# Expert adapter with layer norm: biases broadcast by DMA, W_up loaded by slots, W_down in 4 KB pieces, tail reordered

## The reference

```python
Wd = W_down[stream]; bd = b_down[stream]; Wu = W_up[stream]; bu = b_up[stream]
g = ln_w[stream]; b = ln_b[stream]
h = jnp.einsum('bsh,bhk->bsk', hidden_states, Wd) + bd[:, None, :]     # 512 -> 256
h = jax.nn.gelu(h, approximate=False)
h = jnp.einsum('bsk,bkh->bsh', h, Wu) + bu[:, None, :]                 # 256 -> 512
h = residual + h
mean = jnp.mean(h, axis=-1, keepdims=True)
var = jnp.mean(jnp.square(h - mean), axis=-1, keepdims=True)
h = (h - mean) * jax.lax.rsqrt(var + LN_EPS)
return h * g[:, None, :] + b[:, None, :]
```

## Time and profile before

| | before |
|---|---|
| median of three runs | 143.63 us (143.4 to 145.49) |
| profiled execution | 143.75 us, its span 142.0 us |
| TensorE busy | 126.5 us, 89% |
| VectorE busy | 112.3 us, 79% |
| GpSimd (POOL) busy | 100.9 us, 71% |
| ScalarE busy | 85.7 us, 60% |
| DMA | 21.93 MB, mean 154 GB/s |

### The profile page before, as it was taken

The page is one execution under the profiler, slowest core; times in us unless marked ns, Lnnn a source line. Parts: engine busy times, 40 slices in busy tenths (PEclk is TensorE's granted clock), DMA queues, the critical chain, the costliest instruction groups (busy, mean ns, idle before and its releaser), DMA issues.

```text
span 142.0 us, 4003 instructions
## 1 busy us (share of the span) xinstructions
PE 126.5 (89%) x814; PEld 109.8 (77%) x815; DVE 112.3 (79%) x269; ACT 85.7 (60%) x177; POOL 100.9 (71%) x110
## 2 busy tenths in 40 slices
PE   0399948999999999999999999999999999999800
PEld 0152947999989999898999999999999999998500
DVE  1764449588888888888898888888888978897982
ACT  0763556656666666666666666666766666665320
POOL 3000691055888988888889888888888898889670
PEclk9999999999999999999999999999999999999985
DMA  1959999834325355544553554544446533333346
GB/s 50 359 131 346 282 305 317 210 124 129 115 74 144 90 176 156 150 137 155 145 193 127 170 162 133 167 145 149 149 148 148 148 74 74 79 74 74 74 113 185
DMA packets 13185, 21.93 MB, mean 154 GB/s; under 512 B 2290, under 2 KB 3826, under 8 KB 13172
## 3 DMA queue, kind: packets, MB, share of 16 engines
q1 hardware_dynamic: 8948, 16.01, 39.0%
q10 hardware_dynamic: 4224, 5.79, 13.5%
HBM read 13.39 MB, written 8.65 MB: 155 GB/s over the span
## 4 chain that ended last, share of the span: by engine, by line
PE 83%; DVE 6%; POOL 2%; ACT 2%; DMA 2%; DVEq 1%; issue 1%; POOLq 1%; ACTq 0%
PE hg_ps L733 31%; PE y_ps L758 29%; PE xT_ps L721 10%; PE y_ps L699 5%; PE hg_ps L742 5%; DVE wu_lo L239 2%; POOL res L348 2%; DMA itok_all_i<-in_itok_B_dram 2%; PE hg_ps L695 2%; ACT normed L427 1%; DVEq L568 1%; POOLq L60 1%; ACT wu_hi L437 1%; PE hg_ps L699 1%; DVE hb L586 1%
## 5 line engine op out<-in xcount | busy, mean ns | idle before, releaser
L333 POOL TENSOR_TENSOR xb<-x_sb,bu_rows 128x512 f32<-128x512 f32 x33 | 43.5, 1319 | 13.8 <-ACT bu_rows L449 13.5
L348 POOL TENSOR_TENSOR res<-normed,lnb_rows 128x512 f32<-128x512 f32 x31 | 39.9, 1287 | 15.7 <-ACT normed L427 15.7
L407 ACT ACTIVATE g<-hb 128x256 f32<-128x256 f32 x33 | 13.8, 418 | 36.0 <-DVE hb L586 36.0
L598 DVE BATCH_NORM_STATS2 r_stats<-y_ps 128x6 f32<-128x512 f32 x33 | 23.0, 696 | 8.3 <-issue 7.5
L578 DVE TENSOR_TENSOR xT_lo<-xT_ps,xT_hi 128x512 fp32r<-128x512 f32 x33 | 22.8, 689 | 3.9 <-ACT xT_hi L402 3.9
L619 DVE SCALAR_TENSOR_TENSOR scaled<-y_ps,r_mv,lnw_rows 128x512 f32<-128x512 f32 x33 | 24.5, 743 | 0.1
L733 PE MATMUL hg_ps<-wd_hi,xT_hi 128*128 x132 | 24.2, 306 | 0.0
L758 PE MATMUL y_ps<-wu_hi,gT_hi 128*128 x66 | 23.4, 435 | 0.7 <-ACT gT_hi L412 0.7
L339 POOL TENSOR_TENSOR rstd<-var_eps,half_neg 128x1 f32<-128x1 f32 x33 | 18.5, 562 | 7.1 <-DVE var_eps L607 7.1
L427 ACT ACTIVATE normed<-scaled,rstd 128x512 f32<-128x512 f32 x31 | 22.4, 722 | 1.6 <-DVE scaled L619 1.6
L402 ACT CAST xT_hi<-xT_ps 128x512 fp32r<-128x512 f32 x33 | 18.8, 571 | 4.3 <-PE xT_ps L721 4.3
(11 more groups left out here) (71 smaller groups left out, 136.6 us busy)
## 6 DMA issues: line engine op xcount, KB each, us to landing
x_sb<-in_x_dram SPq DMA_DIRECT2D x66, 128.0 KB, 2.8
out_dram<-res ACTq DMA_DIRECT2D x33, 128.0 KB, 2.4
out_dram<-res SPq DMA_DIRECT2D x33, 128.0 KB, 2.4
wd<-in_L_cond_W_down_dram ACTq DMA_DIRECT2D x3, 512.0 KB, 4.5
wu<-in_L_cond_W_up_dram SPq DMA_DIRECT2D x3, 512.0 KB, 6.1
lnw_rows<-in_L_cond_ln_w_dram SPq DMA_DIRECT2D x1, 768.0 KB, 6.7
lnb_rows<-in_L_cond_ln_b_dram SPq DMA_DIRECT2D x1, 768.0 KB, 7.9
bd_flat<-in_L_cond_b_down_dram SPq DMA_DIRECT2D x1, 3.0 KB
```

Of the source, the lines that this page charges most:

```text
L333: pool.tensor_tensor(xb[:, c % DEEP, :], x_sb[:, c % FAR, :], bu_rows[:, ds(e * H, H)], ALU.add).then_inc(xb_ready, 1)
L348: pool.tensor_tensor(res[:, c % FAR, :], normed[:, c % PAR, :], lnb_rows[:, ds(e * H, H)], ALU.add).then_inc(res_ready, 1)
L598: dve.bn_stats(r_stats[:, c % DEEP, :], y_ps[c % YBANKS][:]).then_inc(stats_ready, 1)
```

## The change

- `b_down` and `b_up` are no longer loaded flat and spread by TensorE. Two DMAs write them to all 128 partitions, `bd_rows` behind W_up of the first slot, `bu_rows` behind x of tile 1. The `spread_row` matmuls and the five ACT copies are gone.
- W_up is loaded by slots: slot 0 gets the expert of the first tile, read from a table, slots 1 and 2 the ones behind it. TensorE's register table `up_down` holds a tile's slot and the next tile's expert. `up(0)` waits for slot 0 only, `up(1)` for all three.
- W_down is loaded as `(p c) n`, four consecutive rows (4 KB) to a partition, where it was `(c p) n`, four pieces of 1 KB. To match, `transpose_x` reads every fourth column of x, `k::KH`.
- TensorE sets the four `y_ps` banks with K=1 float32r matmuls, runs nine warm-ups before the first x transposes and one behind them; `down(0)` waits for the hi halves first and for the lo halves only where it uses them.
- In the sort, a tile's own expert is loaded by a DMA of its own (64 x 4 bytes) where it was taken out of the matrix by a masked sum; steps are reordered, and three small ones build the new tables.
- In the tail, VectorE scales the last tile ahead of `shift_last` of the one before; `last_places` (ACT) and `e_last` (VectorE, two entries for three) are read behind the main loop instead of ahead of it.

Declarations of tiles and semaphores are left out.

```diff
@@ -55,7 +55,7 @@
+    WARM_UPS_BEFORE, WARM_UPS_AFTER = 9, 1
 
@@ -222,10 +218,12 @@
         def load_w_down(eng, e):
-            eng.dma_start(wd[:, e, :, :], w_down[e].rearrange("(c p) n -> p c n", p=P)).then_inc(wd_in[e], 16)
-        def load_w_up(eng, e):
-            eng.dma_start(wu[:, e, :, :], w_up[e].rearrange("(c p) n -> p c n", p=P)).then_inc(wu_in[e], 16)
+            eng.dma_start(wd[:, e, :, :], w_down[e].rearrange("(p c) n -> p c n", p=P)).then_inc(wd_in[e], 16)
+        def load_w_up(eng, slot, e):
+            eng.dma_start(wu[:, slot, :, :], w_up[ds(e, 1), :, :].rearrange("a (c p) n -> p (a c) n", p=P)).then_inc(
+                wu_in[slot], 16)
@@ -243,8 +241,7 @@
         def _(sp):
-            sp.dma_start(bd_flat[:], rows_of(b_down, 1)).then_inc(bd_in, 16)
-            sp.dma_start(bu_flat[:], rows_of(b_up, 1)).then_inc(bu_in, 16)
+            sp.dma_start(itok_own_i[:], itok.rearrange("(p a) -> p a", a=1)).then_inc(itok_in, 16)
@@ -274,13 +271,22 @@
+            def entries_and_expert(t):
+                sp.reg_load(io_regs, io_table[0:1, ds(3 * t, 3)])
+                return ([sp.snap(reg, min_val=0, max_val=B - 1) for reg in io_regs[:2]],
+                        sp.snap(io_regs[2], min_val=0, max_val=E - t))
             load(0, 0, entries(0, 0, 2))
-            load_w_up(sp, 0)
-            load_w_up(sp, 1)
-            load(1, 1, entries(1, 0, 2))
-            load_w_up(sp, 2)
-            load(2, 2, entries(2, 0, 2))
-            load(3, 3, entries(3, 0, 2))
+            sp.wait_ge(slots_ready, 2)
+            for t in range(1, E + 1):
+                batches, e = entries_and_expert(t)
+                load_w_up(sp, t - 1, e + (t - 1))
+                if t == 1:
+                    sp.dma_start(bd_rows[:], rows_of(b_down, P)).then_inc(bd_in, 16)
+                load(t, t, batches)
+                if t == 1:
+                    sp.dma_start(bu_rows[:], rows_of(b_up, P)).then_inc(bu_in, 16)
@@ -310,11 +316,11 @@
-            pool.memset(ones_row[:], 1.0).then_inc(ones_ready, 1)
...
+            pool.iota(top_row[:], pattern=[[-1, E]], base=E - 1, channel_multiplier=0).then_inc(const_ready, 1)
@@ -348,7 +354,7 @@
-            pool.wait_ge(bu_ready, E)
+            pool.wait_ge(bu_in, 16)
             for t in range(DEEP):
@@ -362,9 +368,10 @@
             tiles(pool, body, FAR + 1, TILES - 1 - DEEP)
-            for t in range(TILES - DEEP, LAST):
-                shift(t - 1, t - 1)
-                power(t, t)
+            shift(LAST - 3, LAST - 3)
+            power(LAST - 2, LAST - 2)
+            shift(LAST - 2, LAST - 2)
+            power(LAST - 1, LAST - 1)
             power(LAST, LAST)
@@ -416,6 +423,8 @@
+                else:
+                    act.wait_ge(banks_set, t + 1)
@@ -437,33 +446,19 @@
-            def keep_down_bias(part):
-                act.wait_ge(spread, part + 1)
-                n = bd_banks[part].shape[1]
-                act.copy(bd_rows[:, part * H:part * H + n], bd_banks[part]).then_inc(bd_ready, 1)
-            def keep_up_bias(e):
-                act.wait_ge(spread, len(bd_banks) + e + 1)
-                act.copy(bu_rows[:, e * H:(e + 1) * H], y_ps[e][:]).then_inc(bu_ready, 1)
-            wd_high(0)
-            wd_high(1)
-            keep_down_bias(0)
-            keep_down_bias(1)
-            wd_high(2)
+            act.wait_ge(const_ready, 6)
+            act.copy(marks[:], ident[0:1, 0:1].broadcast_to([1, H])).then_inc(marks_ready, 1)
             for e in range(E):
-                keep_up_bias(e)
+                wd_high(e)
             x_hi(0, 0)
...
             x_hi(1, 1)
+            gelu(0, 0)
             wu_high(1)
-            gelu(0, 0)
-            wu_high(2)
             g_hi(0, 0)
...
             x_hi(2, 2)
+            wu_high(2)
@@ -479,11 +474,11 @@
-            last_places = [place(t) for t in range(TILES - EARLY, TILES)]
             for t in range(1, STORE_B_LAG + 2):
...
+            last_places = [place(t) for t in range(TILES - EARLY, TILES)]
@@ -516,24 +511,22 @@
-            dve.wait_ge(const_ready, 5)
-            dve.wait_ge(itok_in, 16)
+            dve.wait_ge(const_ready, 6)
+            dve.wait_ge(itok_in, 32)
+            dve.tensor_scalar(itok_own[:], itok_own_i[:], 0.0, float(E - 1), ALU.max, ALU.min)
...
-            link(dve.scalar_tensor_tensor(out=own_only[:], in0=itok_all[:], scalar=1.0, in1=ident[0:B, 0:B],
-                                          op0=ALU.mult, op1=ALU.mult, accum_out=itok_own[:]))
-            dve.scalar_tensor_tensor(out=same_before[:], in0=itok_all[:], scalar=itok_own[:], in1=before[:],
-                                     op0=ALU.is_equal, op1=ALU.mult, accum_out=rank[:])
             for e in range(E - 1):
+                dve.tensor_scalar(of_expert[:, e, :], itok_all[:], float(e), None, ALU.is_equal, ALU.add,
+                                  accum_out=count[:, e:e + 1])
+            for e in range(E - 1):
...
-            for e in range(E - 1):
-                last = dve.tensor_scalar(of_expert[:, e, :], itok_all[:], float(e), None, ALU.is_equal, ALU.add,
-                                         accum_out=count[:, e:e + 1])
-            link(last)
+            dve.tensor_scalar(code[:], itok_own[:], float(B), batch_col[:], ALU.mult, ALU.add)
+            link(dve.scalar_tensor_tensor(out=same_before[:], in0=itok_all[:], scalar=itok_own[:], in1=before[:],
+                                          op0=ALU.is_equal, op1=ALU.mult, accum_out=rank[:]))
...
-            dve.tensor_scalar(code[:], itok_own[:], float(B), batch_col[:], ALU.mult, ALU.add)
             link(dve.scalar_tensor_tensor(out=slots_before[:], in0=even_count[:], scalar=-TO_EVEN, in1=behind[:],
@@ -548,8 +541,15 @@
-            dve.tensor_scalar(tile_expert[:], key_filled[:, 1:1 + SLOTS:2], B.bit_length() - 1, RANGE // B - 1,
-                              ALU.logical_shift_right, ALU.bitwise_and).then_inc(slots_ready, 1)
+            first_expert = tile_expert[:, 0:1].broadcast_to([1, E])
+            link(dve.tensor_scalar(tile_expert[:], key_filled[:, 1:1 + SLOTS:2], B.bit_length() - 1, RANGE // B - 1,
+                                   ALU.logical_shift_right, ALU.bitwise_and))
+            dve.tensor_tensor(io_view[:, 1:1 + E, 2], first_expert, top_row[:], ALU.min)
+            pair_view = up_down[:].rearrange("p (t n) -> p t n", n=2)
+            dve.tensor_tensor(pair_view[:, :, 0], tile_expert[:], tile_expert[:, 0:1].broadcast_to([1, TILES]),
+                              ALU.subtract)
+            dve.tensor_copy(pair_view[:, 0:TILES - 1, 1], tile_expert[:, 1:TILES]).then_inc(slots_ready, 1)
@@ -559,8 +559,6 @@
-            dve.wait_ge(slots_ready, 3)
-            e_last = [expert_of(dve, TILES - 1 - i) for i in range(EARLY)]
@@ -571,6 +569,7 @@
+            dve.wait_ge(slots_ready, 2)
@@ -635,14 +634,14 @@
             wu_low(0)
-            dve.wait_ge(bd_ready, len(bd_banks))
+            dve.wait_ge(bd_in, 16)
             down_bias(0, 0)
             x_lo(1, 1)
+            g_lo(0, 0)
             wu_low(1)
-            g_lo(0, 0)
-            wu_low(2)
...
+            wu_low(2)
@@ -667,6 +666,7 @@
             tiles(dve, body, 6, TILES - 3)
+            e_last = [expert_of(dve, TILES - 1 - i) for i in range(2)]
@@ -680,8 +680,8 @@
             variance(last, last)
+            scale(last, last, e_last[0])
...
-            scale(last, last, e_last[0])
@@ -689,36 +689,33 @@
-            def warm_up(times):
+            def warm_up(times, bank):
                 for _ in range(times):
-                    pe.matmul(h_ps[1][:, 0:P], ident[:], ident[:], start=True, stop=True)
-            def spread_row(bank, row):
-                pe.matmul(bank, ones_row[:], row, start=True, stop=True).then_inc(spread, 1)
-            pe.wait_ge(ones_ready, 1)
-            pe.wait_ge(bd_in, 16)
-            spread_row(bd_banks[0], bd_flat[0:1, 0:H])
-            spread_row(bd_banks[1], bd_flat[0:1, H:E * BN])
-            pe.wait_ge(bu_in, 16)
-            for e in range(E):
-                spread_row(y_ps[e][:], bu_flat[0:1, e * H:(e + 1) * H])
+                    pe.matmul(bank[:, 0:P], ident[:], ident[:], start=True, stop=True)
+            pe.wait_ge(marks_ready, 1)
+            for bank in y_ps:
+                pe.matmul(bank[:], marks[:, 0:P], marks[:], start=True, stop=True).then_inc(banks_set, 1)
+            warm_up(WARM_UPS_BEFORE, xT_ps[1])
...
-                pe.reg_load(expert_regs, tile_expert[0:1, ds(t, 2)])
+                pe.reg_load(expert_regs, up_down[0:1, ds(2 * t, 2)])
...
+            def up_slot(t):
+                pe.reg_load(expert_regs[:1], up_down[0:1, ds(2 * t, 1)])
+                return pe.snap(expert_regs[0], min_val=0, max_val=E - 1)
...
                 for k in range(KH):
-                    chunk = slice(k * P, (k + 1) * P)
-                    mm = pe.transpose(xT_ps[c % PAR][:, chunk], x_sb[:, c % FAR, chunk], ident[:])
```

(14 more changed lines are left out.)

16 lines of the change are left out of this document (6 added, 10 removed).

## The result

| | before | after |
|---|---|---|
| median | 143.74 us (4 runs: 143.4 to 145.49) | 147.0 us (4 runs: 146.46 to 147.98) |
| ratio after / before | | 1.021, 95% interval 1.0111 to 1.0308 |
| profiled execution, span | 143.75, 142.0 us | 147.07, 145.3 us |
| x transposes of tile 4, of tile 5 start | 27.67, 31.14 | 28.13, 31.92 |
| one tile from 5 to 32 | 3.465 us | 3.527 us |

A forecast was written before the change was run, and what follows sets the result against it. TensorE's packed stretch was taken as the bound, its start set by head bytes. Span 142.0 - 0.5 (head) + 0 (packed stretch) + 0.4 (tail) = 141.9, plus 1.75, less 0.12: 143.5 us; range 140.3 to 145.9, held at 0.80.

The forecast's parts named there:

- What bounds the kernel: Whole kernel: TensorE never waits from tile 4 to 32, so time changes only in stretch start, time per tile and tail.
- The packed stretch: TensorE's tiles 4 to 32: strided x weight loads taken as 0, bounds 0 and +13.2 us.
- The head: Before tile 4's transposes: packed stretch starts 0.5 us earlier, bounds -0.8 to +1.5 us.
- the broadcasts: Head DMA: 1.18 MB of biases to 128 partitions cost 3.6 us of full queues; tile 4 lands at 27.0.
- The sort: Head: own-expert change ends the sort 0.3 us earlier, bounds 0 (its new load lands late) and 0.42.
- SyncE's work: Head: two more issues cost SyncE 1.2 us, hidden as tile 5 waits 6.7 us in the queues.
- The tail: After the packed stretch: +0.4 us in sum, bounds 0 to +0.7.
- Two loads: Tail: VectorE's two e_last register loads, moved in front of the last body, lie on the path and cost +0.6 us.
- The swap: Tail: scaling the last tile before shift_last of the one before gives back 0.2 us, bounds 0 and 0.4.
- The clock: Rival: TensorE's clock falls while idle in the starved head, up to +1.5 us, 145.0 us; chance 0.12.
- the nine early warm-ups: Head: they should have TensorE at 2.4 GHz by 12 us; tile 0 through its down products at about 14.4 us.
- Strided loads: Rival, packed stretch: x weight loads at half pace cost 0.44 us on 30 tiles, +13.2, 156.7 us; chance 0.17.

The follow-up runs named there:

- f4: Kernel before with W_down in 2 KB pieces and x transposes reading every second float (8-byte step): 146.04 us, ratio 1.008 to before.
- e2: Kernel after with VectorE's two e_last register loads ahead of the main loop again: 146.66 us, ratio 1.014 to before.
- f1: e2 with scale of the last tile behind shift_last of the one before again: 148.11 us, ratio 1.010 to before.
- h1: Kernel after with the own expert by masked sum and W_up loaded by expert, without the second table's wait and third entry: 146.68 us, ratio 1.011 to before.
- f3: Kernel before with six more warm-up matmuls behind tile 1's x transposes: 144.39 us, ratio 0.998 to before.
- e1: Kernel after with W_down in four 1 KB pieces and contiguous x transposes again: 145.97 us, ratio 1.005 to before.
- e3: Kernel after with the own expert by the masked sum again instead of its own DMA: 146.24 us, ratio 1.012 to before.
- g2: Kernel after with W_up loaded by expert again, without the wait for the second table and the third entry: 147.62 us.
- h2: Twin of h1, e3's kernel run again: kernel after with the masked sum alone, 146.08 us, ratio 1.007 to before.

## Why the prediction was wrong, by its own steps

**What bounds the kernel: right.** TensorE's packed stretch, the start and the tail are the three places, and the whole 3.3 us are found there.

**The packed stretch: the step that failed.** I took 0 for the strided weight loads "as the nearest row does". That row was VectorE's read of 33 int32, and it was near in name only: another engine, one partition, and at 0.16 us so short that a price per element could not show. f4 makes it plain, since the very 8-byte step that the row has costs a TensorE weight load 67 ns. The measured term is 0.05 to 0.07 us a tile, 1.7 of the +2.0 us in the trace of after, against bounds of 0 and 13.2; 0.3 is the first step behind a wait. The lower bound was right as a bound and wrong as a choice, and all or nothing between the two ends left out what came: a load half as long again, mostly hidden. Four loads of 141 ns, 564 in all, already stood in transposes of 440 ns; from that I could have asked how much of a longer load fits beside the matmuls.

The Trainium skill, "Advanced Engine Details and Errata", section "SBUF Cachelines", was right that a step of 16 bytes carries a penalty (209 ns for 140). Its 16-byte line with two hits needed would let the 8-byte step go free; f4's 208 ns don't agree, and the measurement decides.

**The head: right in its bytes, wrong in what stands in front of them.** -0.5 was forecast, +0.46 came (-0.2 to +0.5 in the traces of after, e2 and f1). With neither the small DMA nor the table read, h1 takes tile 4 at 26.70, straight from its DMA, for a forecast of 27.0. As its sort gained nothing (first x issue at 7.51 for 7.54), the broadcasts cost 3.0 us there (26.7 for 23.7), less than my 3.6; it is the fastest of twelve executions, so part of the agreement is luck. Tile 5 was never waited for, neither in it nor in after. Two terms failed. The sort was to end 0.3 us earlier, with 0 as the bound for a late small DMA; it began 0.62 later, behind a late list, and the first x load was issued 0.41 later (7.95 for 7.54). And SyncE's work was called hidden, "as tile 5, now issued last at 20.6, waits 6.7 us in the queues". That is true of the last issue and false of the first: W_up's first slot is issued at 10.13 for 8.88, 0.84 us later even when counted from the first x issue, behind 0.68 us of register load and its wait, into queues at a share of 0.3 to 0.7. I had counted what SyncE issues and left out what it reads.

**The tail: right in its mechanism.** Two loads were to cost 0.6 and cost 0.59. The swap was to give back 0.2 and gives 0. With the 0.26 on top whose cause is open, +0.4 became +0.85. The three misses, 2.0, 0.96 and 0.45, are 3.4 of the 3.5 us between 143.5 and 147.0.

**The clock: right that it is there, wrong on whose it is.** I asked whether the change would lose it and read "the clock stayed at 1.00" off one trace of before. The kernel before loses it itself, going by f3, in most executions (47 of 72). A trace of one execution couldn't show that; the times 143.4, 143.6 and 145.49 could have raised the question. The changed head loses it too, in five of the nine traces that have it (e1, e2, e3, g2, h2), though at tile 4 it costs little where bytes are late. And the nine early warm-ups didn't have TensorE at full speed by 12 us: the transposes of tile 0 at 12.42 still take 1.06 us, and `down(0)` ends at about 16.1 for the 14.4 of the forecast; the head's bytes, which bind, hid that.

**Chances.** Strided loads were the rival that ended slower, at 0.17 and 156.7 us. That mechanism was the largest miss, at about a seventh of that price; nothing between 0 and 13.2 had been given a chance.

## What to carry to other kernels

A row is near to an unknown operation only if it has the same engine and enough elements for the price to show; where no such row exists, give the middle of the bounds a chance instead of choosing an end. In a head bound by bytes, ask of every issue not how long it takes but whether the queues are full while it is late; the first load behind a pause is the one that nothing in the queues covers. And look at the single times before the median: two levels mean a hidden state that a change can enter or leave, worth nearly 2 us here, more than half of what the change costs.
